# State-stage inputs as two 64-row tiles into two PSUM banks, with the logits in another bank

## The reference, cut to what matters

```python
h = tok(x, positions, ...)                      # (16, 128, 64)
h = h + attn(layernorm(h), ...)                 # the state stage
h = h + ffn(layernorm(h), ...)                  # hidden 256, 8 experts, top-1

# attn: complex poles, written as a recurrence over the 128 positions
u = x @ B_bar.real.T + 1j * (x @ B_bar.imag.T)
h = causal_convolution(u, A_powers)             # h[t] = A_bar * h[t-1] + u[t]
y = (h @ (C_real + 1j * C_imag).T).real
# ffn
H = gelu(x @ W1 + b1); probs = softmax(H @ Wg + bg); out = probs[e] * (H @ Wd[e] + bd[e]), e = argmax
```

## Time and profile before

| | us |
|---|---|
| median of 3 runs | 112.52 (112.30 to 113.85) |
| the profiled execution, its time | 112.29 |
| the profiled execution, its span | 110.5 |
| TensorE busy | 100.0 |
| VectorE busy | 89.0 |
| ScalarE busy | 70.8 |
| GpSimd busy | 52.9 |

### The profile page before, as it was taken

The page is one execution under the profiler, slowest core; times in us unless marked ns, Lnnn a source line. Parts: engine busy times, 40 slices in busy tenths (PEclk is TensorE's granted clock), DMA queues, the critical chain, the costliest instruction groups (busy, mean ns, idle before and its releaser), DMA issues.

```text
span 110.5 us, 2010 instructions
## 1 busy us (share of the span) xinstructions
PE 100.0 (90%) x717; PEld 64.4 (58%) x723; DVE 89.0 (81%) x230; ACT 70.8 (64%) x126; POOL 52.9 (48%) x101
## 2 busy tenths in 40 slices
PE   5989999999999798789899999999999799999930
PEld 2356785364334476247666677976777476667610
DVE  0369999999969949999998799498999926498871
ACT  4604599999999999999779349156746606431000
POOL 7799999898986008007329254544005000000940
PEclk9999999999999999999999999999999999999995
DMA  3999700000000100000000000000000000000142
GB/s 90 264 244 407 270 0 0 3 0 0 6 0 3 5 1 0 0 0 6 0 0 0 0 0 6 0 0 0 0 3 6 0 0 0 0 0 0 33 98 59
DMA packets 4297, 4.15 MB, mean 38 GB/s; under 512 B 3264, under 2 KB 3520, under 8 KB 4160
## 3 DMA queue, kind: packets, MB, share of 16 engines
q1 hardware_dynamic: 4144, 3.92, 12.5%
q10 hardware_dynamic: 144, 0.12, 0.4%
HBM read 3.50 MB, written 0.52 MB: 36 GB/s over the span
## 4 chain that ended last, share of the span: by engine, by line
PE 44%; ACT 38%; DVE 5%; DMA 4%; issue 3%; POOL 2%; ACTq 0%
PE pair L1079 17%; ACT wave L475 8%; PE bank L1041 7%; ACT bell L465 7%; ACT bell L469 5%; ACT L424 5%; DMA ids<-x 4%; PE hid_pair L1052 3%; PE pair L950 3%; ACT angle L513 3%; ACT h L459 2%; PE hid_pair L1062 2%; ACT dist L454 2%; PE pair L920 2%; PE pair L1086 2%
## 5 line engine op out<-in xcount | busy, mean ns | idle before, releaser
L378 POOL TENSOR_SCALAR var_eps<-mean_var 128x4 f32<-128x4 f32 x8 | 3.7, 458 | 31.0 <-DVE mean_var L746 30.9
L818 DVE COPY_PREDICATED pair<-later,pair 128x256 f32<-128x256 int32 (+3 forms) x30 | 12.3, 410 | 5.9 <-PE pair L1079 5.2
L920 PE MATMUL pair<-warm 128*128 128x512 bf16 x49 | 12.4, 379 | 0.5 <-issue 0.5
L731 DVE SCALAR_TENSOR_TENSOR bell<-bell,scale_w,wave 128x512 f32<-128x512 f32 x16 | 11.0, 754 | 1.1 <-ACT wave L475 1.1
L1079 PE MATMUL pair<-wd_high,H_high 128*128 128x512 f32 x32 | 10.8, 418 | 0.0
L920 PE MATMUL hid_pair<-warm 128*128 128x512 bf16 x28 | 8.9, 474 | 1.5 <-POOL warm L297 1.3
L394 POOL TENSOR_TENSOR angle<-picked,prob 128x256 f32<-128x256 f32 x3 | 1.8, 613 | 17.2 <-DVE prob L842 17.2
L1079 PE MATMUL pair<-wd_low,H_high 128*128 128x512 f32 x32 | 10.0, 394 | 0.0
L520 ACT ACTIVATE bell<-hid_pair,sm 128x512 f32<-128x512 f32 x8 | 5.0, 680 | 7.2 <-PE hid_pair L1052 7.2
L674 DVE TENSOR_TENSOR wave<-dist,inv_width 128x2048 f32<-128x2048 f32 x4 | 9.1, 2298 | 0.0
L964 PE MATMUL pair<-h,w_sb 128*64 128x512 f32 x40 | 9.0, 597 | 0.0
(11 more groups left out here) (166 smaller groups left out, 228.4 us busy)
## 6 DMA issues: line engine op xcount, KB each, us to landing
ids<-x SPq DMA_DIRECT2D x2, 512.0 KB, 5.7
posb<-positions SPq DMA_DIRECT2D x1, 768.0 KB, 8.0
wd_sb<-wd SPq DMA_DIRECT2D x1, 512.0 KB, 9.2
out<-angle SPq DMA_DIRECT2D x4, 128.0 KB, 2.0
st_sb<-state SPq DMA_DIRECT2D x1, 328.0 KB, 8.3
w_sb<-w SPq DMA_DIRECT2D x1, 256.0 KB, 6.6
posb<-positions SPq DMA_DIRECT2D x1, 256.0 KB, 6.6
w_sb<-w SPq DMA_DIRECT2D x1, 160.0 KB, 8.0
```

The source lines that it names most:

```text
L731: ins = dve.scalar_tensor_tensor(out=bell[:, g, part], in0=bell[:, g, part], scalar=scale_w[:, s:s + 1], in1=wave[:, g, part], op0=ALU.mul ...
L818: return dve.copy_predicated(held[:, :, 0:n, 0, 0:D], repeat(later[:, g, 2 * h + rows.start:2 * h + rows.stop, first:first + n], 3, D), he ...
L920: pe.matmul(bank[free], warm[:, 0:P], warm[:, :], start=True, stop=True)
```

## The change

The state inputs become two products on 64 rows each: sequences of the upper rows go to `mid_pair` bank 0, those of the lower rows to bank 1, each in columns 256 to 511. `mid_pair` is the old bank 4 (`state_bank`) and bank 5 (`layer_bank`) as one tensor. The transposes keep columns 0 to 255 of bank 4 and the outputs columns 0 to 255 of bank 5. The logits move from bank 5 to columns 0 to 127 of bank 4. Waits keep the operations on a shared bank apart: `inputs_in(g)` waits for an `s_hb` count (1, 1 and 3 for groups 1 to 3), `outputs(g)` for `s_drive` (3, 3 and 4), and `logits_back` for all four `s_drive`, in place of `s_hb`; `outputs(3)` no longer waits for `s_lread`. `logits_back(0)` moves behind `hidden(1)` and `route(0)` behind `scan(3)`.

```diff
-        bank += [ctx.enter_context(nc.psum_tensor(f"bank{i}", [P, T], F32))[:, :] for i in range(4, 6)]
+        mid_pair = ctx.enter_context(nc.psum_tensor("mid_pair", [P, 2, T], F32))
+        bank += [mid_pair[:, i, :] for i in range(2)]
...
-        logit_cols = layer_bank[:, 2 * P:3 * P].rearrange("p (j e) -> p j e", e=GATE)
+        states_in = mid_pair[:, :, 2 * P:4 * P]
+        logit_cols = state_bank[:, 0:P].rearrange("p (j e) -> p j e", e=GATE)
...
-                dve.tensor_tensor(drive[:, g, :].rearrange("p (b t) -> p b t", b=GB),
-                                  state_bank.rearrange("p (b t) -> p b t", b=GB),
-                                  repeat(drive_tab, 1, GB), ALU.mult).then_inc(s_drive, 1)
+                dve.tensor_tensor(drive[:, g, :].rearrange("p (h c t) -> p h c t", h=2, c=2),
+                                  states_in.rearrange("p h (c t) -> p h c t", c=2),
+                                  repeat(repeat(drive_tab, 1, 2), 1, 2), ALU.mult).then_inc(s_drive, 1)
...
-            route(0)
             driven(3)
             scan(3)
+            route(0)
             turn_back(3)
...
                 if g == 0:
                     pe.wait_ge(ld["state"], 16)
+                    pe.wait_ge(s_amps, 2)
                 pe.wait_ge(s_xT[0], g + 1)
+                if g:
+                    pe.wait_ge(s_hb, (1, 1, 3)[g - 1])
                 for h in range(2):
-                    mm = pe.matmul(state_bank[:, h * 2 * P:(h + 1) * 2 * P], B_rows[h],
-                                   xT[:, g].rearrange("p b t -> p (b t)"), start=True, stop=True)
+                    rows = slice(h * D, (h + 1) * D)
+                    mm = pe.matmul(states_in[:, h, :], B_rows[h][rows, :],
+                                   xT[rows, g].rearrange("p b t -> p (b t)"), start=True, stop=True)
...
-            def outputs(g, routed=0):
+            def outputs(g):
...
                 if g:
                     pe.wait_ge(s_hb, g)
-                if routed:
-                    pe.wait_ge(s_lread, routed)
+                    pe.wait_ge(s_drive, (3, 3, 4)[g - 1])
...
-            def logits_back(g, added):
+            def logits_back(g):
                 pe.wait_ge(s_gcopy, g + 1)
-                pe.wait_ge(s_hb, added)
+                pe.wait_ge(s_drive, G)
...
             experts_high(0, 1)
-            logits_back(0, 3)
             turn(1, 1)
             inputs_in(3)
             hidden(1)
+            logits_back(0)
```

More of the change, by code:

```diff
@@ L1168, in _ @@
             turn(1, 2)
-            outputs(3, 1)
+            outputs(3)
             hidden(2)
-            logits_back(1, 4)
+            logits_back(1)
             experts_high(1, 0)
@@ L1175, in _ @@
             turn(1, 3)
-            logits_back(2, 4)
+            logits_back(2)
             experts_high(1, 1)
@@ L1183, in _ @@
             experts_high(2, 1)
-            logits_back(3, 4)
+            logits_back(3)
             experts_low(2, 1)
```

## The result

The changed kernel takes 113.0 us (median of 20 runs, 112.68 to 116.44) where the kernel before takes 112.47 us (20 runs): a ratio of **1.0037, 95% interval 1.002 to 1.0054**, some 0.4 us slower. The forecast was 112.9 us.

A forecast was written before the change was run, and what follows sets the result against it. The prediction took the chain of waits to bound the kernel, any delay of gate(1) reaching the end undiminished. 112.29 + 0.49 + 0.0 to 0.1 gave 112.8 us; set between 112.8 and 113.0, it forecast 112.9, range 112.0 to 114.0.

The forecast's parts named there:

- The step: At outputs(1): it must wait for VectorE's driven(2) and starts at 65.40 instead of 64.91, 0.49 us late.
- the first wait: Ahead of inputs_in(1): it waits for residual(0), starts 1.06 us later, and field(3) behind it comes 0.62 us late.
- The sum: Whole kernel: 112.29 + 0.49 + 0.0 to 0.1 = 112.8 us, against the profiled execution.
- The cheaper product: State-input stages on TensorE: 0.62 us, or 0.56 us in front of hidden, saving 0.3 to 0.4 us each.
- The bound of nothing saved: State-input stages: saving 0 if the row tiles do not overlap or the way in and out eats it.
- The tie at outputs(3): At outputs(3): turn_back(3) with hand-over and TensorE both arrive at 79.86; cost 0, up to 0.1 us.
- Rival 1: At scan(3): the scan comes before GpSimd's offset of group 1, 2, which loses 1.0 us; 113.9 us, chance 0.13.
- Rival 2: Near 59.2 us: GpSimd's L378 comes before scan(1), VectorE is up to 1 us sooner; 112.3 us, chance 0.15.
- Rival 3: State-input stages: tiles run one after the other or the way in and out eats the saving; 113.6 us, chance 0.07.
- rival 4: TensorE idles over 1 us before 57.55 and the granted clock falls; over 114 us, chance 0.03.

The follow-up runs named there:

- e4_route_alone: The kernel before with only route(0) moved behind scan(3) and logits_back(0) behind hidden(1), old banks, products and waits: 112.91 us, ratio 1.0047.
- The first experiment: The changed kernel with driven(2) called ahead of moments(0, 3) on VectorE, nothing else: 113.73 us, ratio 1.0114 to the kernel before.

## Why the prediction was right

**The reading that carried it.** That TensorE's time ahead of `turn(1, 0)` is lost in waits, that `outputs(1)` is fixed by VectorE's order at 64.61 + 0.66 + 0.13, and that nothing between there and `gate(1)` becomes cheaper: each holds within 0.02 us in the table. The step was shown by its removal, once with another bank (0.999) and once by a later scan (0.9986), both with the first wait still in place. That `turn(1, 0)` is late by exactly the 0.40 us of the forecast is luck: `inputs_in(1)` started 0.14 us behind the end of `residual(0)`, not 0.03, and `field(3)` came 0.75 us late instead of 0.62; the 0.4 was picked below that bound. The sum did not rest on it.

**The cheaper product.** 0.64 and 0.54 us against the 0.62 and 0.56 of the forecast. The way in costs 0.09 us, about the 0.1 us allowed: from the start of `turn(1, 0)` to the stage there are 0.31 us, and 0.22 us with the old products in the new places (63.69 to 63.91). The bound of nothing saved is excluded by the old products with the new places, whose stage takes 0.95 us. The stage is 0.1 us longer where other work follows than in front of `hidden` (0.64 against 0.54), but so was the old product (1.06 against 0.96), so this is not the price of the way out of the tile form, as the forecast had it. "TensorEngine Tiling (Array Packing)", Key Properties, of the Trainium skill says that changing the tiling mode drains TensorE; the traces agree with a cost of 0.09 us on the way in and show next to none on the way out.

**The tie at outputs(3)** fell on the good side: `driven(3)` started 0.06 us sooner than worked out (75.55 against 75.61) and `turn_back(3)` 0.19 us sooner, the rest because `route(0)` starts 1.14 us behind the scan's start (76.59 to 77.73) and I had put it at 1.25. It cost nothing.

**The rivals.** Rival 1 was 0.14 us away (76.45 against 76.59) and is real: an input 0.2 us earlier brought it about and cost 0.93 us. Its condition was worked out too loosely: a saving of 0.5 us instead of 0.35 would have put the scan at 76.19, still behind the offset at 76.14. Rival 2 is real too, but I gave it wrongly: having line 378 first is not enough, the root behind it must be first as well, which takes a scan about 0.3 us later rather than 0.02 us (0.27 us was too little with three small instructions, 0.35 us enough with the old products in the new places). The 0.15 that I gave it was too much for a kernel in which `driven(1)` keeps its time. Rival 3 is excluded. The clock (rival 4) stayed at full in this stretch, with TensorE idle for 1.26 us at one place.

**What I missed without harm.** From `gate(1)` on TensorE was said to have next to no gap, and it idles 0.57 us at 87.24. The delay passes it undiminished because `normalise(1, 3)`, which it waits for, stands behind `gate_out(2)` on ScalarE and is as late as `gate(2)` is: 0.58 us are idle there in the changed kernel. The replaced wait of `logits_back(1)` I called "not last". With `route(0)` moved it would have been, by 0.23 us (e4_route_alone); that it was replaced is a part of the change that pays. My number for the moved calls alone, 1.001 to 1.002, was wrong for this reason. The first experiment shows the same gap in looking: I checked GpSimd against VectorE where the prediction needed it, not where I moved work.

## What to carry to other kernels

A cheaper instruction is worth what the first wait behind it leaves of it: follow it to the next point where its engine waits for another, and ask which engine sets that time. When a layout puts more tenants into a bank, price the waits by the time at which the other tenant is through, and look for a bank that is idle just then. Where one engine can hold up another, as VectorE's scan does GpSimd's small instructions, order on the scale of 0.1 us decides about 1 us, so before moving a call list what the other engine has on at its new place.

## What the runs showed of the hardware

Who starts first decides whether VectorE holds GpSimd. A GpSimd instruction of 0.20 or 0.23 us on SBUF that starts 0.02 to 0.25 us behind a VectorE instruction of 1.2 us with two SBUF operands (the scan, or the difference `wd_low`) takes 0.99 to 1.23 us. One that starts 0.14 us ahead of a scan (76.45 against 76.59 in the changed kernel) takes its usual 0.20 us, and the scan its 1.23 us. A root of 1.02 us that started 0.02 us (the old products in the new places) or 0.19 us (five small instructions) ahead of a scan took its 1.02 us, and the scans took 1.26 and 1.21 us against 1.22; one that started 0.07 us behind it took 1.96 us. `driven`, which reads PSUM and SBUF, held nobody: in the changed kernel line 380 starts at 65.10, 0.18 us behind `driven(2)`, and takes 0.23 us. The Trainium skill, "SBUF — State Buffer", Who interferes with whom, says that a VectorE instruction with two SBUF inputs contends with a GpSimd instruction that reads SBUF, and that the order of issue decides who blocks. The lines agree where GpSimd comes second; that neither is held where the root comes first is what the traces add.

The time outside the span was 2.2 us in the median of two kernels (the old products with the new places, and the Gelu moved) and 1.8 to 2.0 in that of all others. Single executions spread from 1.7 to 3.2 us, and no trace shows what decides this.
